# Key attention of a fused four-layer network: the LayerNorm of x applied by ScalarE as scale and shift

## What is computed

```python
def _layernorm(x, axis=-1, eps=1e-05):
    m = jnp.mean(x, axis=axis, keepdims=True)
    v = jnp.var(x, axis=axis, keepdims=True)
    return (x - m) / jnp.sqrt(v + eps)
...
def _L0_ffn_ref(x, Wq, Wk, Wv, Wo, Wff):
    q, k, v = split_heads(x @ Wq), split_heads(x @ Wk), split_heads(x @ Wv)
    scores = jnp.einsum('bqd,bkd->bkq', q, k) / jnp.sqrt(jnp.asarray(D, x.dtype))
    attn = jax.nn.softmax(scores, axis=-1)
    out = jnp.einsum('bkq,bkv->bqv', attn, v)
    z = out.reshape(B, H, S, dh).transpose(0, 2, 1, 3).reshape(B, S, L)
    z = _l2_normalize(_l2_normalize(z @ Wo) @ Wff)
    return jax.nn.gelu(z, approximate=False)
...
x = x + _L0_ffn_ref(_layernorm(x, axis=-1), L0_ffn_Wq, ...)
```

## Time and profile before

| | |
|---|---|
| median of 3 runs | 1939.39 us (1938.0 to 1941.11) |
| the profiled execution | 1931.33 us |
| its span from the first to the last instruction | 1929.5 us |
| mean granted TensorE clock over the span | 0.824 of full speed |
| busy over the span | TensorE 1413.2 us, VectorE 1179.1, ScalarE 738.6, GpSimd 580.2 |
| the stage in question | about 245 to 425 us of the span |

### The profile page before, as it was taken

The page is one execution under the profiler, slowest core; times in us unless marked ns, Lnnn a source line. Parts: engine busy times, 40 slices in busy tenths (PEclk is TensorE's granted clock), DMA queues, the critical chain, the costliest instruction groups (busy, mean ns, idle before and its releaser), DMA issues. The chain is left out here.

```text
span 1929.5 us, 44227 instructions
## 1 busy us (share of the span) xinstructions
PE 1413.2 (73%) x14920; PEld 1093.4 (57%) x14920; DVE 1179.1 (61%) x3476; ACT 738.6 (38%) x1845; POOL 580.2 (30%) x1074
## 2 busy tenths in 40 slices
PE   6999989865999842499947999843299565576563
PEld 3777645543777642388836888633288444454353
DVE  4888569978888653144423555464111179969896
ACT  2666546754666532122213555400133222232232
POOL 4555211112110056200037653046300286201221
PEclk9999957876999855699978999955699867687577
DMA  4322200000000001366631110001377411010001
GB/s 157 119 103 107 87 1 2 3 3 17 22 22 19 11 33 38 108 178 180 179 98 44 42 41 27 12 22 43 92 201 198 116 42 30 1 33 12 1 1 44
DMA packets 111125, 120.10 MB, mean 62 GB/s; under 512 B 12656, under 2 KB 88432, under 8 KB 110832
## 3 DMA queue, kind: packets, MB, share of 16 engines
q1 hardware_dynamic: 102768, 101.15, 18.0%
q0 software_dynamic: 8192, 16.79, 3.1%
HBM read 81.19 MB, written 36.70 MB: 61 GB/s over the span
## 5 line engine op out<-in xcount | busy, mean ns | idle before, releaser
L2342 PE MATMUL e_H<-e_xT,e_w_up 128*128 128x256 f32 x736 | 177.7, 390 | 11.2 <-DMA e_w_up<-in_f_dram 9.4
L2342 PEld LDWEIGHTS e_H<-e_xT,e_w_up 128*128 128x128 f32 x736 | 136.8, 194 | 34.8 <-issue 16.4
L2270 DVE COPY e_xT<-e_pX 128x256 f32<-128x256 f32 x72 | 30.6, 425 | 188.9 <-PE e_pX L2331 188.9
L2352 PE MATMUL e_pY<-e_w_down,e_h 128*128 128x128 f32 x992 | 124.8, 277 | 11.6 <-ACT e_h L2319 10.8
L2352 PEld LDWEIGHTS e_pY<-e_w_down,e_h 128*128 128x128 f32 x992 | 119.5, 192 | 24.3 <-issue 16.6
L2177 POOL DMA_INDIRECT slots_in<-R,r_put x96 | 92.7, 966 | 55.4 <-issue 30.6
L2308 ACT ACTIVATE e_silu<-e_H 128x256 f32<-128x256 f32 x120 | 46.1, 384 | 143.4 <-PE e_H L2342 143.4
L430 DVE TENSOR_REDUCE a_mx<-a_S 128x8 f32<-128x1024 f32 x64 | 78.2, 1221 | 32.5 <-PE a_S L515 32.3
L475 ACT ACTIVATE a_PT<-a_ST 128x1024 f32<-128x1024 f32 x64 | 65.6, 1025 | 77.7 <-PE a_ST L542 77.7
L2277 DVE TENSOR_TENSOR e_h<-e_silu,e_H 128x256 f32<-128x256 f32 x120 | 50.6, 421 | 69.5 <-ACT e_silu L2308 69.5
L2331 PE MATMUL e_pX<-W,e_rows 128*128 128x128 f32 x144 | 28.7, 282 | 80.4 <-DMA e_rows<-slots_in 79.2
(11 more groups left out here) (416 smaller groups left out, 4123.7 us busy)
## 6 DMA issues: line engine op xcount, KB each, us to landing
slots_in<-Y SPq DMA_DIRECT2D x32, 512.0 KB, 3.2
e_w_up<-in_f_dram SPq DMA_DIRECT2D x40, 384.0 KB, 3.4
e_w_down<-in_f_dram SPq DMA_DIRECT2D x32, 322.0 KB, 3.0
e_rows<-slots_in SPq DMA_DIRECT2D x72, 128.0 KB, 2.4
slots_out<-e_y SPq DMA_DIRECT2D x72, 128.0 KB, 3.3
e_w_up<-in_f_dram SPq DMA_DIRECT2D x32, 256.0 KB, 3.7
e_w_down<-in_f_dram SPq DMA_DIRECT2D x40, 192.0 KB, 2.8
a_cK<-in_ctxT_dram SPq DMA_DIRECT2D x64, 64.0 KB, 1.8
```

Of the source, the lines that this page charges most:

```text
L2342: i = nc.tensor.matmul(H[:, banks * p + b, CHUNK * c:CHUNK * (c + 1)], up[:, p, at:at + P], xT[:, p, :], start=True, stop=True)
L2352: i = nc.tensor.matmul(pY[:, D * s:D * s + D], h[:, p, c, P * s:P * s + P], down[:, p, D * c:D * (c + 1)], start=(c == 0), stop=(c == HC - 1))
```

## The change

ScalarE makes xn as `Identity(rstd * x + shift)` with a scale and a bias per token, at the end of its iteration u+1 (lag 1, the last of its list). GpSimd makes the shift, -mean * rstd, in two more 128x1 operations behind its two others. VectorE's apply (lag 2) is gone. A 128x1 constant of -1 is set once by GpSimd; VectorE's first wait counts it too. xn, its buffers and its readers stay the same.

```diff
         ln = LayerNorm(net, sb, sem, xn, s_xt)
+        minus, shift, one = sb("minus", [P, 2]), sb("shift", [P, 2]), sb("one", [P, 1])
+        s_minus, s_shift = sem("minus_mean"), sem("shift")
...
             nc.gpsimd.memset(V[:], 0.0).then_inc(s_zero, 1)
-
-            pipeline(pool, NT, [(1, lambda u, p: ln.pool_rstd(pool, u, p))],
-                     straight=True)
+            nc.gpsimd.memset(one[:, :], -1.0).then_inc(s_zero, 1)
+            pool.wait_ge(s_zero, 2)
+
+            def rstd_and_shift(u, p):
+                ln.pool_rstd(pool, u, p)
+                nc.gpsimd.tensor_tensor(minus[:, p:p + 1], ln.moments[:, p, 0:1], one[:, :], ALU.mult
+                                        ).then_inc(s_minus, 1)
+                done(pool, s_minus, u)
+                done(pool, ln.s_rstd, u)
+                nc.gpsimd.tensor_tensor(shift[:, p:p + 1], minus[:, p:p + 1], ln.rstd[:, p, 1:2], ALU.mult
+                                        ).then_inc(s_shift, 1)
+
+            pipeline(pool, NT, [(1, rstd_and_shift)], straight=True)
...
-            dve.wait_ge(s_zero, 1)
+            dve.wait_ge(s_zero, 2)
...
-            pipeline(dve, NT, [(2, lambda u, p: ln.vector_apply(dve, u, p)), (5, softmax(0)), (5, softmax(1)),
+            pipeline(dve, NT, [(5, softmax(0)), (5, softmax(1)),
                                (1, lambda u, p: ln.vector_moments(dve, u, p)),
                                (0, lambda u, p: ln.vector_stats(dve, u, p)), (7, divide_v)], straight=True)
...
+            def apply(u, p):
+                done(act, s_shift, u)
+                free(act, s_xt, u)
+                nc.scalar.activation(xn[:, p, :], X[:, u, :], ACT.Identity, bias=shift[:, p:p + 1],
+                                     scale=ln.rstd[:, p, 1:2]).then_inc(ln.s_xn, 1)
+
...
-            pipeline(act, NT, [(10, take_z), (6, exps), (3, take_qkv), (4, spread_q), (11, squares), (2, take_xt)],
+            pipeline(act, NT, [(10, take_z), (6, exps), (3, take_qkv), (4, spread_q), (11, squares), (2, take_xt), (1, apply)],
                      straight=True)
```

## The result

The changed kernel takes 1946.78 us (median of 16 runs, 1942.12 to 1950.92), the kernel before, run alongside it, 1937.81 us (1932.04 to 1941.80): ratio 1.0049, interval 1.0036 to 1.0061, +9.0 us. Forecast were 1939.6 us and a range up to 1945.5.

The account below looks back on a forecast made before the run. TensorE bounds at the half clock, VectorE at the mostly full clock. VectorE's saving -4.4, dips +3.4, fill +0.5 and +0.7 sum to +0.2 us on the median of 1939.39: 1939.6 us, range 1933.0 to 1945.5.

Parts of the forecast that it names:

- The loop does not bind: Wait of ScalarE's apply for the aggregate, through all engines: 8.80 us for two tiles, under VectorE's 9.30.
- TensorE's lead in a steady tile: How long scores(1) are ready before VectorE's maximum reads them: forecast to shrink from 2.1 to 0.5 us.
- The fill of the pipeline: Start of the stage: first xn later, +0.5 us, and slower first tiles, +0.7 us (between 0 and 1.5).
- At a dip of the clock TensorE slows: At the half clock TensorE's work per tile goes from 3.66 to 6.07 us; dips cost 4.8 us after the change.
- Before, its lead hid much of this: In the kernel before, VectorE lost only 0.8 and 0.6 us in the two long dips, 1.4 in all.
- dips of the kernel before: Two long and two shorter falls of the clock, 309 to 395 us: 4.8 us after against 1.4 before, +3.4.
- -4.4: VectorE without xn: 0.25 us saved a tile over 17.5 tiles between 309 and 395 us, in us.
- The idle time that TensorE had for xn becomes one for take_qkv: TensorE's wait before the transpose: it would wait for ScalarE's take_qkv instead of VectorE's xn; no size given.
- fewer dips: Rival, chance 0.23: a denser TensorE keeps the clock up from 309 us on, -4.6 us, 1934.8 us.
- The rule of the Trainium skill on VectorE's saturation: Where VectorE is saturated, moving work to ScalarE may pay: 0.25 us on all 30 full tiles, -7.5 us.
- The loop closes: Rival, chance 0.17, at ScalarE's apply: decides from about 0.7 us more in the loop; +4.1 us, 1943.5 us.
- The Trainium skill's rule of short idle times that make the clock swing: Short idle times between groups of TensorE's matmuls make the clock swing; fewer gaps, fewer swings; no size of its own.

Follow-up runs that it names:

- apply_behind_exp: The changed kernel with ScalarE's apply at lag 2, behind the exponential and ahead of take_qkv: 1923.64 us, ratio 0.9964 to the kernel before.
- after_output_twice: The changed kernel with TensorE's output projection issued twice where it stands, ahead of scores(1): 1929.44 us, ratio 0.9960 to the kernel before.
- apply_first_lag2: The changed kernel with ScalarE's apply at lag 2, after take_z and ahead of the exponential: 1936.53 us, ratio 1.0005 to the kernel before.
- after_output_behind: The changed kernel with TensorE's output projection moved behind scores(1), issued once: 1929.54 us over six runs, ratio 0.9964 to the kernel before.
- after_output_behind_2: A second group of runs of the changed kernel with the output projection behind scores(1), issued once: 1943.24 us, ratio 0.9975 to the kernel before.

## Why the prediction was wrong

Right, step by step: V to maximum is 0.21 us and a tile at the full clock 4.65. The two multiplies take 0.19 us each. No table load. The apply starts 1.53 us after the aggregate (1.62 forecast), its length of 0.49 us against 0.40 is hidden, and scores(0) follows 4.72 us after the aggregate (4.86). TensorE's lead in a steady tile is 0.70 us (0.5 forecast). The loop does not bind at a steady clock. The fill of the pipeline: from the first `bn_stats` to the tenth aggregate it took 39.75 us, in the trace before 38.13, +1.6 against 1.2.

Wrong was one step, "At a dip of the clock TensorE slows" and "Before, its lead hid much of this": I priced the *dips of the kernel before*, two long and two short, in a kernel with another idle pattern, and gave +3.4 us for them. What the runs show in its place is +11.8 us of waiting for scores from 309 us on (17.3 in the whole stage, of which 5.9 lie in the fill). With 11.8 for 3.4 the forecast's own sum comes to -4.4 + 11.8 + 0.5 + 0.7 = +8.6 us, near the 9.0 measured. The kernel before was priced well, 1.4 us against 1.6; it is the dips after the change, 4.8 us against 14.5 and 12.4, that were not. The prediction had the sentence "The idle time that TensorE had for xn becomes one for take_qkv" and put no price on it. The step missing was to follow a *late* tile, not a steady one, around the loop: an aggregate that is 0.9 us late makes take_qkv 0.9 us late for a TensorE that is already back at the full clock. The steady tile has 1.0 us of idle time, the late one 1.5. The long stretches at the half clock add to it: they cover 42 us in the first profile where the kernel before had 24 of its long dips, and a tile in them mostly costs VectorE 1.33 us of waiting.

Of the rivals, "fewer dips" argued that 3.66 / 4.65 is denser than 3.66 / 4.90. A clock that stays up is what apply_behind_exp and after_output_twice show, and then the change does not lose; but the density did not bring it in the changed kernel. The rule of the Trainium skill on VectorE's saturation (Perfetto Trace Analysis, Optimizing Scalar/DVE Operations) gave -7.5 us. apply_behind_exp's 0.9964 is -7 us, but part of that is the better clock: with the clock held in both kernels the difference was 2.6 to 3.8 us, about half of what the rule gave. "The loop closes" named the right place, ScalarE's apply, and the wrong condition: it needs no 0.7 us more, since a stall closes it. The Trainium skill's rule of short idle times that make the clock swing (TensorE: Matmul & The Clock Gate, A second HAM failure mode) agrees with the changed kernel's alternation at 1.53 us and with the falls of the kernel before behind pieces of 0.94 us, and does not with apply_behind_exp's steady 1.02.

The sum of the whole stage as measured: -8 us of VectorE's work, +17 us of its waits, +9 us, half a per cent.

Open: why the clock rises at 288 us in one execution and at 309 in another, what makes the clock fall behind one idle piece and not behind the next (see the last section), and why apply_first_lag2 is better than the changed kernel by more than its 0.15 us.

## What to carry to other kernels

Work moved to an engine with idle time brings its *wait* with it: put it in that engine's queue where its operand is already there, behind the work that others wait for, not ahead of it. Here that one place in a list was the difference between +0.5% and -0.4% of the kernel before. When a kernel lives near a change of TensorE's clock, follow one late tile around the loop as well as a steady one, and look at the windows of the granted clock before believing a sum of durations.

## What the runs showed of the hardware that was not expected

TensorE at the half clock can show as busy for every microsecond and stay there: 24.00 of 24 us in the earlier trace rows, and in after_output_behind from 285 to 369 us, at 6.18 us a tile. A second issue of the same matmul (0.4 us at the full clock) stood in eight profiled executions; from 285 us on no stretch at the half clock lasted beyond 313 us in any of them, and from 316 to 392 us the clock did not fall in any. The kernels without it were not all worse: in after_output_behind_2 the clock stayed at 1.00 from 285 us on. A busy share of 1 in the profile is not by itself a sign that the clock will rise.

In the changed kernel an idle piece of 1.53 us that ended at 304.02 was followed by the half clock from about 305.2 us on, and one of 1.72 us that ended at 324.71 by a granted clock of 0.83 in the window of 325 to 326 us and 0.50 in the next. In its two profiles all 14 pieces of 1.38 us or more between 285 and 400 us were followed by a fall. But the length of a piece alone does not order the cases. Of the 14 pieces of 1.02 us in apply_behind_exp one was followed by a fall, of the 13 pieces of 0.94 us in the two profiles of the kernel before seven were (that kernel idles 0.30 us more a tile in a second piece), and one of 1.35 us in apply_first_lag2, which ended at 316.59, was not.
